# Cross-attention in eight batches: a staging buffer for each input, both loaded a batch ahead, and sixteen moves in one piece

## The reference

```python
q = jnp.einsum('bcn,dc->bnd', x1, Wq) + bq
k = jnp.einsum('bcn,dc->bdn', x2, Wk) + bk[:, None]
v = jnp.einsum('bcn,dc->bdn', x2, Wv) + bv[:, None]
attn = jax.nn.softmax(jnp.einsum('bnd,bdm->bnm', q, k), axis=2)
attn_out = jnp.einsum('bcm,bnm->bcn', v, attn)
return attn_out + x1
```

## Time and profile before

| | us |
|---|---|
| median of 3 runs | 693.22 |
| lowest and highest run | 687.25 and 695.76 |
| the profiled execution, its time | 693.22 |
| the profiled execution, its span | 691.4 |

### The profile page before, as it was taken

How to read it: one execution, slowest core, us unless ns; L and a number is a source line. 1 busy time by engine, 2 the same in 40 slices (tenths; PEclk the granted TensorE clock), 3 DMA queues, 4 the chain that set the end, 5 groups by cost and what they waited for, 6 DMA issues and landing times.

```text
span 691.4 us, 8378 instructions
## 1 busy us (share of the span) xinstructions
PE 658.2 (95%) x2848; PEld 537.5 (78%) x2848; DVE 470.8 (68%) x510; ACT 281.8 (41%) x367; POOL 122.1 (18%) x51
## 2 busy tenths in 40 slices
PE   5999799998999999999899998999989998999998
PEld 3877578886888878888688886888868887788886
DVE  4889558696486774886757865679658695586641
ACT  5564432455235352354333732336333364324220
POOL 0302300053001430033200440005300063000200
PEclk9999989999999999999999999999999999999999
DMA  9400931849228482376715585154941749316261
GB/s 317 184 1 17 258 108 61 214 126 250 79 86 227 113 242 91 103 215 165 191 54 146 172 216 159 61 139 153 241 138 61 185 136 240 106 64 164 64 179 63
DMA packets 94874, 100.04 MB, mean 145 GB/s; under 512 B 8336, under 2 KB 69776, under 8 KB 94864
## 3 DMA queue, kind: packets, MB, share of 16 engines
q1 hardware_dynamic: 94864, 99.91, 50.6%
HBM read 51.64 MB, written 16.78 MB: 99 GB/s over the span
## 4 chain that ended last, share of the span: by engine, by line
PE 68%; SPq 13%; DMA 7%; DVE 6%; ACT 3%; issue 2%; ACTq 0%
PE acc_ps L726 30%; PE acc_ps L695 25%; SPq L208 11%; DMA pt_raw<-blocks 6%; PE s_ps L665 5%; PE s_ps L673 4%; PE s_ps L674 4%; DVE blocks L497 2%; SPq L184 2%; DVE probs L488 2%; DVE pt_lo L446 1%; ACT probs L333 1%; ACT pt_hi L298 1%; ACT xs_hi L298 1%; DMA stage<-in_ctx_dram 1%
## 5 line engine op out<-in xcount | busy, mean ns | idle before, releaser
L726 PE MATMUL acc_ps<-pt_hi,vt_hi 128*128 128x512 f32 x512 | 202.7, 396 | 20.7 <-DVE pt_lo L446 20.7
L726 PE MATMUL acc_ps<-pt_lo,vt_hi 128*128 128x512 f32 x512 | 202.0, 395 | 0.0
L726 PE MATMUL acc_ps<-pt_hi,vt_lo 128*128 128x512 f32 x512 | 201.5, 394 | 0.0
L726 PEld LDWEIGHTS acc_ps<-pt_hi,vt_hi 128*128 128x128 f32 x512 | 97.5, 191 | 44.2 <-DVE pt_lo L446 23.6
L333 ACT ACTIVATE probs<-s_ps,negmax 128x1024 f32<-128x1024 f32 x64 | 71.5, 1117 | 128.3 <-DVE negmax L481 128.3
L726 PEld LDWEIGHTS acc_ps<-pt_hi,vt_lo 128*128 128x128 f32 x512 | 97.7, 191 | 20.8
L726 PEld LDWEIGHTS acc_ps<-pt_lo,vt_hi 128*128 128x128 f32 x512 | 97.6, 191 | 20.4
L267 POOL TENSOR_TENSOR pt_lo<-pt_raw,pt_hi 128x1024 fp32r<-128x1024 f32 x14 | 41.0, 2946 | 381.5 <-ACT pt_hi L298 381.5
L695 PE MATMUL acc_ps<-wv_hi,xs_hi 128*128 128x512 f32 x256 | 100.0, 390 | 0.0
L695 PE MATMUL acc_ps<-wv_hi,xs_lo 128*128 128x512 f32 x256 | 99.6, 389 | 0.0
L695 PE MATMUL acc_ps<-wv_lo,xs_hi 128*128 128x512 f32 x256 | 99.6, 389 | 0.0
(11 more groups left out here) (49 smaller groups left out, 613.8 us busy)
## 6 DMA issues: line engine op xcount, KB each, us to landing
pt_raw<-blocks SPq DMA_DIRECT2D x240, 128.0 KB, 2.4
stage<-in_ctx_dram SPq DMA_DIRECT2D x32, 512.0 KB, 5.8
o_sb<-in_x_dram SPq DMA_DIRECT2D x64, 256.0 KB, 3.2
out_dram<-o_sb SPq DMA_DIRECT2D x64, 256.0 KB, 2.5
stage<-in_x_dram SPq DMA_DIRECT2D x28, 512.0 KB, 6.2
blocks<-in_x_dram SPq DMA_DIRECT2D x4, 512.0 KB, 8.4
pt_raw<-in_L_xattn_Wv_dram SPq DMA_DIRECT2D x4, 256.0 KB, 7.8
pt_raw<-in_L_xattn_Wk_dram SPq DMA_DIRECT2D x1, 128.0 KB, 3.5
```

Of the source, the lines that this page charges most:

```text
L726: mm = nc.tensor.matmul(acc_ps[:, c % BANKS, :], v[:, m, cols], p[:, m, :], start=(m == 0 and v is vt_hi and p is pt_hi), stop=(m == MT - ...
```

## The change

Each input gets its own staging buffer, `stage1` and `stage2`, with its own semaphores `s_in1` and `s_in2`. Both buffers of batch b + 1 are loaded at the top of `batch(b)`, first `x1`, then `x2`, each chunk as soon as the low part of the same input of batch b is made. `move(b, 1)` follows with all four quadrants in one piece. Batch 0's `x1` goes into `stage1` and not into `blocks`; a wait of VectorE for it ahead of the first `turn` goes. The size of a scratch area for dynamic DMAs is set to 2048, which leaves room for the second buffer. The orders of ScalarE, VectorE, GpSimd and TensorE stay. The core of the diff (left out are renamings of `stage` to `stage1` or `stage2` in `round_x2`, `low_x1`, `low_x2` and the prologue):

```diff
-        stage = sb("stage", [P, KT, N], F32)
+        stage1 = sb("stage1", [P, KT, N], F32)
+        stage2 = sb("stage2", [P, KT, N], F32)
...
-        x0_raw = blocks[:].rearrange("p (k a) t r -> p k (a t r)", k=KT)
...
-            def load(src, b, k):
-                sp.dma_start(stage[:, k, :], src[b, k * P:(k + 1) * P, :]).then_inc(s_in[k], 16)
+            def load_x1(b, k):
+                sp.dma_start(stage1[:, k, :], x1_d[b, k * P:(k + 1) * P, :]).then_inc(s_in1[k], 16)
+
+            def load_x2(b, k):
+                sp.dma_start(stage2[:, k, :], x2_d[b, k * P:(k + 1) * P, :]).then_inc(s_in2[k], 16)
...
-            def move(b, h, quadrants=range(NQ)):
-
-                if 0 in quadrants:
-
-
-                    sp.wait_ge(s_blk, half_of(b, h) * NT + NT)
-                for i in quadrants:
+            def move(b, h):
+
+                sp.wait_ge(s_blk, half_of(b, h) * NT + NT)
+                for i in range(NQ):
...
+            def next_x1(b, k):
+                sp.wait_ge((s_x1lo_e, s_x1lo_o)[k % 2], b * 2 - 2 + k // 2 + 1)
+                load_x1(b, k)
+
             def next_x2(b, k):
-                sp.wait_ge((s_x1lo_e, s_x1lo_o)[k % 2], b * 2 + k // 2 + 1)
-                load(x2_d, b, k)
+                sp.wait_ge((s_x2lo_e, s_x2lo_o)[k % 2], b * 2 - 2 + k // 2 + 1)
+                load_x2(b, k)
...
                 if not last:
                     for k in range(KT):
-                        sp.wait_ge((s_x2lo_e, s_x2lo_o)[k % 2], b * 2 + k // 2 + 1)
-                        load(x1_d, nb, k)
-                move(b, 1, range(0, 2))
-                if not last:
+                        next_x1(nb, k)
                     for k in (0, 2, 1, 3):
                         next_x2(nb, k)
-                move(b, 1, range(2, NQ))
+                move(b, 1)
...
             def round_x1(b, k):
-                act.wait_ge(s_in[k], b * 32)
-                copy(xs_hi[:, k, :], stage[:, k, :]).then_inc(s_x1hi, 1)
+                act.wait_ge(s_in1[k], b * 16 + 16)
+                copy(xs_hi[:, k, :], stage1[:, k, :]).then_inc(s_x1hi, 1)
...
-            dve.wait_ge(s_x1lo_e, 2)
             turn(0, 4, first=True)
...
-    nc = _bacc.Bacc("TRN2", target_bir_lowering=False, num_devices=1)
+    nc = _bacc.Bacc("TRN2", target_bir_lowering=False, num_devices=1, dynamic_dma_scratch_size=2048)
```

More of the change, by code:

```diff
@@ L117, in build @@
         s_wv = [sem(f"s_wv_{k}") for k in range(KT)]
-        s_x0 = [sem(f"s_x0_{k}") for k in range(KT)]
-        s_in = [sem(f"s_in_{k}") for k in range(KT)]
+        s_in1 = [sem(f"s_in1_{k}") for k in range(KT)]
+        s_in2 = [sem(f"s_in2_{k}") for k in range(KT)]
         s_res = [sem(f"s_res_{i}") for i in range(OUTS)]
@@ L242, in _ @@
             for k in range(KT):
-                load(x2_d, 0, k)
+                load_x2(0, k)
                 if k == 0:
@@ L249, in _ @@
             for k in range(KT):
-                sp.dma_start(x0_raw[:, k, :], x1_d[0, k * P:(k + 1) * P, :]).then_inc(s_x0[k], 16)
+                load_x1(0, k)
                 if k == 0:
@@ L276, in _ @@
                 pool.wait_ge(s_x1hi, k + 1)
-                low(x0_lo[:, k, :], x0_raw[:, k, :], x0_hi[:, k, :]).then_inc(s_x1lo_e, 1)
+                low(x0_lo[:, k, :], stage1[:, k, :], x0_hi[:, k, :]).then_inc(s_x1lo_e, 1)
             def p_lo(b, j):
@@ L286, in _ @@
                     pool.wait_ge(s_x1hi, b * KT + KT + k + 1)
-                    low(xs_lo[:, k, :], stage[:, k, :], xs_hi[:, k, :]).then_inc(s_x1lo_e, 1)
+                    low(xs_lo[:, k, :], stage1[:, k, :], xs_hi[:, k, :]).then_inc(s_x1lo_e, 1)
                 for i, k in enumerate((0, 2)):
                     pool.wait_ge(s_x2hi, b * KT + KT + i + 1)
-                    low(xs_lo[:, k, :], stage[:, k, :], xs_hi[:, k, :]).then_inc(s_x2lo_e, 1)
+                    low(xs_lo[:, k, :], stage2[:, k, :], xs_hi[:, k, :]).then_inc(s_x2lo_e, 1)
                 p_lo(b + 1, 1)
@@ L300, in round_x1 @@
             def round_x1(b, k):
-                act.wait_ge(s_in[k], b * 32)
-                copy(xs_hi[:, k, :], stage[:, k, :]).then_inc(s_x1hi, 1)
+                act.wait_ge(s_in1[k], b * 16 + 16)
+                copy(xs_hi[:, k, :], stage1[:, k, :]).then_inc(s_x1hi, 1)
             def round_x2(b, k):
-                act.wait_ge(s_in[k], b * 32 + 16)
-                copy(xs_hi[:, k, :], stage[:, k, :]).then_inc(s_x2hi, 1)
+                act.wait_ge(s_in2[k], b * 16 + 16)
+                copy(xs_hi[:, k, :], stage2[:, k, :]).then_inc(s_x2hi, 1)
             def cross_rows(slot):
@@ L400, in _ @@
             for k in range(KT):
-                act.wait_ge(s_in[k], 16)
-                copy(xs_hi[:, k, :], stage[:, k, :]).then_inc(s_x2hi, 1)
+                act.wait_ge(s_in2[k], 16)
+                copy(xs_hi[:, k, :], stage2[:, k, :]).then_inc(s_x2hi, 1)
                 if k == 0:
@@ L414, in _ @@
                     v_hi(0, 0)
-                act.wait_ge(s_x0[k], 16)
-                copy(x0_hi[:, k, :], x0_raw[:, k, :]).then_inc(s_x1hi, 1)
+                act.wait_ge(s_in1[k], 16)
+                copy(x0_hi[:, k, :], stage1[:, k, :]).then_inc(s_x1hi, 1)
             v_hi(0, 1)
@@ L472, in low_x1 @@
                 dve.wait_ge(s_x1hi, b * KT + k + 1)
-                sub(xs_lo[:, k, :], stage[:, k, :], xs_hi[:, k, :]).then_inc(s_x1lo_o, 1)
+                sub(xs_lo[:, k, :], stage1[:, k, :], xs_hi[:, k, :]).then_inc(s_x1lo_o, 1)
             def low_x2(b, k):
                 dve.wait_ge(s_x2hi, b * KT + (1 if k == 0 else 4 if k == 3 else 3))
-                sub(xs_lo[:, k, :], stage[:, k, :], xs_hi[:, k, :]).then_inc((s_x2lo_e, s_x2lo_o)[k % 2], 1)
+                sub(xs_lo[:, k, :], stage2[:, k, :], xs_hi[:, k, :]).then_inc((s_x2lo_e, s_x2lo_o)[k % 2], 1)
             def neg_max(b, t):
@@ L612, in _ @@
                 dve.wait_ge(s_x1hi, k + 1)
-                sub(x0_lo[:, k, :], x0_raw[:, k, :], x0_hi[:, k, :]).then_inc(s_x1lo_o, 1)
+                sub(x0_lo[:, k, :], stage1[:, k, :], x0_hi[:, k, :]).then_inc(s_x1lo_o, 1)
                 v_lo(0, k // 2)
```

## The result

The changed kernel took 671.8 us (median of 4 runs, 671.2 to 672.4), the kernel before beside it 694.5 us. The ratio is 0.969, with a 95% interval of 0.962 to 0.976. The forecast was 673.3 us and 2.9% less. The profiled execution has a span of 670.4 us, 21.0 less than the 691.4 before.

The account below looks back on a forecast made before the run. TensorE, busy 658.2 of 691.4 us, was taken as the bound, losing time to late pt_lo and a lowered clock. Waits -13.65 and clock -6.3 gave a 671.5 us span, plus 1.8 profiled-run excess: 673.3 us, range 665 to 682.

Parts of the forecast that it names:

- The moves: SyncE, second half: sixteen moves without loads between issue in 10.52 us, so pt_hi could start 12.42 us after their start.
- T: Time at which SyncE starts the moves of a batch's second half; 398.50 in batch 4 before the change.
- The loads cost nothing where they went: Four x2 loads behind the x1 loads fill idle DMA, ending 1 us before the second half's moves; costed at 0.
- What is late next: VectorE's written-out order then holds pt_lo; TensorE still waits 1.0 us in each of seven second halves; waits -13.65 us.
- The clock: TensorE's clock stays full behind waits under 1.50 us in the second halves: -6.3 us.
- The second rival: TensorE's clock still falls, since idle length alone doesn't decide: 680 us, 14%.
- The sum: Whole kernel: waits -13.65 and clock -6.3 give -19.95 us, span 671.5 us, run 673.3 us, 2.9% less.
- the third rival: SyncE's queue: the moves stand behind eight loads and land late, making the kernel slower, 729 us at 145 GB/s; 3%.
- the moves have 5.8 us of slack: Second half: pt_hi may start as late as 18.2 us after the moves start, against 12.4 expected, without delaying VectorE.
- one of the signs named for being right: ScalarE no longer waits for the moves before pt_hi of a second half of the loop, but for s_used.
- the other batches repeat this: The five other loop batches after the first follow batch 4, each keeping 1.0 us of TensorE's wait.
- the chain: VectorE's q_low, low_x2(1), out(0, 2), low_x2(3), then p_lo: TensorE starts 11.87 us after q_cross.

Follow-up runs that it names:

- The first experiment: Changed kernel with its two buffers but the old SyncE order (eight moves, four x2 loads, eight moves): 689.4 us, ratio 0.999 to the kernel before.
- the second: Kernel before with its one buffer, the sixteen moves in one piece and the x2 loads behind them: 725.2 us, ratio 1.051 to the kernel before.
- the GpSimd experiment: Changed kernel with GpSimd subtracting only 8 of 1024 columns of chunk 2 of x2: 663.9 us, ratio 0.962 to the kernel before.
- the reordering: Changed kernel with VectorE's four p_lo ahead of low_x2(3): 665.0 us, ratio 0.965 to the kernel before; repeated on one chip, 664.7 us.
- the added operations: Changed kernel with one or two more VectorE operations ahead of p_lo in batches 0 to 6: 682.4 us with one, 697.8 us with two.
- the fourth experiment: Changed kernel with SyncE issuing the four x2 loads only after s_blk, right ahead of the sixteen moves: 681.9 us, ratio 0.989 to the kernel before.

## Why the prediction was right

**The moves.** Right: sixteen issues take 10.55 us, and the last move of batch 4 lands some 12.3 us behind T (issued at T + 9.9, 2.4 us on its way); T + 12.42 was forecast for the time by which `pt_hi` can start. The first experiment shows that this is the place of the loads and not the buffer; the second, that the buffer is what lets them leave it.

**The loads cost nothing where they went.** Right by time (over at T - 1.4), and no `round_x1` waits for its load in the loop. One small miss: the four `x2` loads took 3.23 us to issue and not 1.9, hidden in 10 us of idle queue.

**What is late next.** Right to 0.01 us: seven waits of 0.99 us for 1.0, by VectorE's order; the GpSimd experiment and the reordering take them away, and the added operations lengthen them one for one.

**The clock.** Right for the changed kernel: -6.3 us in the profile, with no half slow. The second rival's point that length alone doesn't decide was right too. Over the nine profiles here that have such waits, TensorE's clock had fallen behind the wait in 0 of 25 cases of 0.98 to 1.81 us, 1 of 8 of 2.0 to 2.1, 4 of 11 of 2.2 to 2.6, 7 of 8 of 3.0 to 3.3, and 11 of 11 above 5. What else than length decides between 2.0 and 3.3 us was not found.

**The sum.** -13.65 - 6.3 = -19.95 us was forecast and the span fell by 21.0. Waits gave 20.7 - 6.9 = 13.8, the clock behind them 6.3. The other 0.9 was not in the sum: it lies in the prologue, where TensorE's pace doubled some 2 us earlier. Windows of before, then of after, at the same place:

```profile
13.50:15.70 2.20, 2.20 (x6) 1.71 (x6) 1.58 (x3) 0.31 (x2) 0.00 (x0) 1.00 1.04 408
```

```profile
13.50:15.70 2.20, 2.20 (x11) 1.82 (x10) 1.72 (x3) 1.35 (x2) 0.00 (x0) 1.00 1.02 400
```

With 6 matmuls started in one and 11 in the other, I read it as the clock's first rise, from 1.2 to 2.4 GHz, although this column says 1.00 for both; that reading isn't shown. That it is chance and no part of the change, the other profiles bear out. The first 12 matmuls of the k projection took 5.49 us before and 4.53 after; they took 5.46 and 5.49 in two kernels with the change (GpSimd cut short, `p_lo` first), and 4.71 and 4.35 in the two with the one old buffer (scratch size alone, moves in one piece). So the change itself is worth 20.1 us of the 21.0, for 19.95 forecast.

**Where it was wrong.** In the third rival: "the moves have 5.8 us of slack" was worked out in batch 4 and is true of batches 1 to 6. Batch 0, whose q projection comes 4.5 us earlier after its turns, has about 1 us. For the same reason one of the signs named for being right did not show in batch 0: ScalarE still waited 2.25 us for the moves there, and `p_lo` came no later for it only because of that 1 us. That did not touch the forecast, since the queue was empty at T, but it is most of why the fourth experiment's expectation failed. The step that failed is "the other batches repeat this", taken over from the chain, where I had looked at batch 0 by itself, to the slack, where I had not.

## What to carry to other kernels

When a load stands among latency-bound transfers, ask whether a buffer would let it be issued where the queue is empty, and cost the pair: here the buffer alone gave nothing that could be told (0.1%), the unbroken moves alone cost 5%, and both together gave 3.1%. Then look at what is late next; the wait that is left can be an engine's written-out order, and swapping two of its operations was worth another 1.2%. A threshold worked out in a steady batch has to be worked out again for the first one.

## What the runs showed of the hardware

GpSimd and VectorE, each subtracting two buffers, take turns: `low_x2(1)` went from 3.32 to 1.23 us when the GpSimd operation beside it was cut to 8 columns, and nothing else was changed. The Trainium skill (SBUF — State Buffer, "Who interferes with whom") states such a lock; this run shows its price here, 2.1 us for that operation and 7.9 us for the kernel.

Behind seven waits of equal length (2.11 us) in one execution TensorE's clock fell once and stayed full six times. The kernel before, whose waits lie about that region, also has the widest scatter of times of the three kernels compared here, and its clock goes with it (mean granted clock 0.985 in its run of 698.3 us, 0.990 in that of 689.8): its runs beside the last experiments lay between 689.8 and 698.3 us, those of the changed kernel between 671.6 and 673.1, and those with `p_lo` first between 664.4 and 665.5.
